# Cross-attention and routed experts on one core: a new call order, with stores spread and a bias moved

## The reference

```
h    = layernorm(x)
q,k,v = h Wq + bq, ctx Wk + bk, ctx Wv + bv            16 heads of 16
s    = alpha * 4 * (q.k) / (|q| + |k|)^2
x    = x + softmax(s) v Wo + bo
g    = layernorm(x);  p = softmax(g Wr)                8 experts
w    = the two largest of p, scaled to sum 1
x    = x + sum over the two chosen e of w_e (gelu(g W1[e] + b1[e]) W2[e] + b2[e])
```

## Time and profile before

| | us |
|---|---|
| median of 3 runs | 1087.3 (1085.24 to 1088.91) |
| the profiled execution, its own time | 1081.77 |
| its span, first to last instruction | 1080.0 |
| TensorE busy in the span | 957.4 (89%) |
| VectorE busy | 700.8 (65%) |
| ScalarE busy | 586.2 (54%) |
| GpSimd busy | 455.0 (42%) |

### The profile page before, as it was taken

The page is one execution under the profiler, slowest core; times in us unless marked ns, Lnnn a source line. Parts: engine busy times, 40 slices in busy tenths (PEclk is TensorE's granted clock), DMA queues, the critical chain, the costliest instruction groups (busy, mean ns, idle before and its releaser), DMA issues. The chain is left out here.

```text
span 1080.0 us, 27856 instructions
## 1 busy us (share of the span) xinstructions
PE 957.4 (89%) x9394; PEld 822.2 (76%) x9394; DVE 700.8 (65%) x1777; ACT 586.2 (54%) x978; POOL 455.0 (42%) x579
## 2 busy tenths in 40 slices
PE   2799999989989989899897159999999999999993
PEld 1588887867868868688676049889898989898982
DVE  5367787866867858668576436656666565656561
ACT  0478887976868758778585033433333333434340
POOL 4225548555564665544545401333333333323232
PEclk9699999998989989899899569999999999999997
DMA  4202223222231333233314456333332333233222
GB/s 131 75 27 80 66 80 106 81 66 71 80 105 32 129 124 114 73 109 103 129 25 170 120 190 259 61 61 54 49 52 46 57 48 54 46 49 55 26 26 25
DMA packets 64437, 87.86 MB, mean 81 GB/s; under 512 B 9360, under 2 KB 57872, under 8 KB 62128
## 3 DMA queue, kind: packets, MB, share of 16 engines
q1 hardware_dynamic: 48016, 64.95, 18.7%
q0 software_dynamic: 14304, 18.92, 10.7%
q10 hardware_dynamic: 1984, 2.21, 0.8%
HBM read 50.94 MB, written 34.06 MB: 79 GB/s over the span
## 5 line engine op out<-in xcount | busy, mean ns | idle before, releaser
L1415 POOL DMA_INDIRECT out<-yw,rb x78 | 132.8, 1703 | 321.6 <-DVE yw L1384 147.7
L1343 ACT ACTIVATE h<-s_ps,b1t,inv 128x256 f32<-128x256 f32 x156 | 79.5, 560 | 232.3 <-PE s_ps L1299 229.6
L1367 DVE SCALAR_TENSOR_TENSOR hs<-h,hsc,hs 128x512 f16<-128x512 f32 x156 | 117.5, 753 | 5.6
L1299 PE MATMUL s_ps<-xt,w1s 128*128 128x256 f16 x936 | 109.5, 274 | 0.0
L1299 PE MATMUL u_ps<-xt,w1s 128*128 128x256 f16 x936 | 108.6, 273 | 0.0
L648 ACT ACTIVATE pt<-gen,escale 128x512 f32<-128x512 f32 x128 | 85.8, 682 | 41.2 <-PE gen L434 20.8
L1314 PE MATMUL pv_ps<-w2s_sb,hs 128*128 x960 | 108.1, 273 | 0.0
L902 DVE SCALAR_TENSOR_TENSOR tw<-th,s_ps 128x1024 f32<-128x1024 f32 x64 | 77.9, 1217 | 38.5 <-PE s_ps L417 20.8
L1314 PE MATMUL gen<-w2s_sb,hs 128*128 x912 | 102.7, 273 | 0.0
L1314 PEld LDWEIGHTS pv_ps<-w2s_sb,hs 128*128 128x128 f16 x960 | 93.9, 98 | 10.9
L1365 DVE TENSOR_SCALAR hs<-h,hsc 128x512 f16<-128x512 f32 x156 | 76.5, 490 | 36.4 <-ACT h L1343 27.0
(11 more groups left out here) (234 smaller groups left out, 1798.6 us busy)
## 6 DMA issues: line engine op xcount, KB each, us to landing
wl<-L_ffn_W SPq DMA_DIRECT2D x16, 1024.0 KB, 5.9
rb<-xrec SPq DMA_DIRECT2D x39, 265.0 KB
w2s<-wst SPq DMA_DIRECT2D x8, 1024.0 KB, 8.8
w2s_sb<-w2s SPq DMA_DIRECT2D x8, 1024.0 KB, 16.6
xin<-x SPq DMA_DIRECT2D x32, 128.0 KB, 3.7
cin<-ctx SPq DMA_DIRECT2D x32, 128.0 KB, 2.1
xres<-x SPq DMA_DIRECT2D x32, 128.0 KB, 4.2
out<-x SPq DMA_DIRECT2D x32, 128.0 KB, 2.0
```

Of the source, the lines that this page charges most:

```text
L1299: ins = pe.matmul(hbank[q][:, o:o + SLOT], w, xt[s % 2][:, xp, k, :], start=(t == 0), stop=(t == len(terms) - 1))
L1343: ins = act.activation(h32[q][:, m % HB, :], hbank[q][:, o:o + SLOT], ACT.Gelu, scale=inv1[:, bass.ds(ex, 1)].bitcast(F32), bias=b1t[:, ba ...
L1367: dve.scalar_tensor_tensor(lo, h, scale, hi, ALU.mult, ALU.subtract).then_inc(sig("lo"), 1)
L1415: pool.indirect_dma_start(out[:, :], bass.IndirectOffsetOnAxis(ap=rb[j][:, i, D + NE:D + NE + 1], axis=0), yw[s % 2][:, i, :], None, compu ...
```

## The change

In the diff, in five parts:

1. `scatter(t, i, p)` issues one store; its eight calls stand at eight places of GpSimd's loop, with `scatter(0, 0)` at the end of one turn and the other seven spread over the next.
2. `add_bias` and `xb` go. bo is split in three bf16 parts (`bop`), and `project_out` begins with a product of ones with `bop` into the same bank. VectorE prepares `bop` at the start.
3. ctx is passed to the kernel with tokens in the columns; `cin` is then used by `project` as it is, in two buffers for each b, and TensorE's `norm` turns x alone.
4. `counts` is a function of its own, called before `shares`; `racc` comes before `rtok` in the chain of semaphore counts.
5. `TURNS` and the loops of all five engines have a new order.

```diff
 def norm(b, p):
     g = pe_turn(pe, f"xct{b}", p)
     pe.wait_ge(*at(f"xn{b}", p + 1))
-    pe.wait_ge(*dma(f"ldc{b}", p + 1))
-    for i, src in enumerate((xn[b], cin[b])):
-        for k in range(DC):
-            o = (DC * i + k) * P
-            ins = pe.transpose(g[:, o:o + P], src[:, k * P:(k + 1) * P], idf[:, :])
+    for k in range(DC):
+        ins = pe.transpose(g[:, k * P:(k + 1) * P], xn[b][:, k * P:(k + 1) * P], idf[:, :])
 def project(b, p):
...
-    for i, w in ((0, wq_sb), (1, wk_sb)):
-        for k in range(DC):
-            ins = pe.matmul(g[:, i * D:(i + 1) * D], xct[b][:, DC * i + k, :], w[:, k, :], ...)
+    for k in range(DC):
+        pe.matmul(g[:, 0:D], xct[b][:, k, :], wq_sb[:, k, :], start=False, stop=False)
+    pe.wait_ge(*dma(f"ldc{b}_{p % 2}", p // 2 + 1))
+    for k in range(DC):
+        ins = pe.matmul(g[:, D:2 * D], cin[b][:, p % 2, k, :], wk_sb[:, k, :], ...)
 def project_out(b, p):
     g = pe_turn(pe, f"wo{b}", p)
+    pe.matmul(g[:, 0:D], ones_b[0:RROWS, :], bop[:, :], start=True, stop=False)
     pe.wait_ge(*at("ote", 2 * p + b + 1))
```

SyncE's turn, and the part of VectorE's turn that reads from it:

```diff
 for it in range(-3, NP + 1):          # SyncE; each call guarded by its own range
-    load(1, it + 2)
-    load_weights(it)
+    residual(0, it)
+    store_x1(0, it - 1)
     store_w2(it - 1)
-    residual(1, it)
+    load_weights(it)
     load(0, it + 3)
-    residual(0, it + 1)
-    store_x1(0, it - 1)
     flat_rows(it + 1)
     store_x1(1, it - 1)
+    residual(1, it)
+    load(1, it + 3)
```

More of the change, by code:

```diff
@@ L90, in build @@
     turns = [(what, it + d, freed, (it + d) // 2 + 1 if what == "rank" else it + d + 1 if b is None else 2 * (it + d) + b + 1)
-             for it in range(-1, NP + 3) for what, d, freed, b in TURNS
+             for it in range(-1, NP + 4) for what, d, freed, b in TURNS
              if 0 <= it + d < NP and (what != "rank" or (it + d) % 2)]
@@ L505, in weight_sum @@
                 pe.matmul(g[:, 0:1], ones_f[:, :], wss[:, :], start=True, stop=True).then_inc(sig("wsum"), 1)
-            for it in range(-1, NP + 3):
+            for it in range(-1, NP + 4):
+                if 0 <= it - 1 < NP:
+                    stack(1, it - 1)
                 if 0 <= it - 2 < NP:
                     turn_on(0, it - 2)
+                    turned(2, 1, it - 2)
+                if 0 <= it - 4 < NP and it % 2:
+                    ranks(it - 4)
                 if 0 <= it - 1 < NP:
@@ L552, in tensor_program @@
                 if 0 <= it - 1 < NP:
-                    weight_products(it - 1)
-                    values(1, it - 1)
+                    turned(1, 1, it - 1)
+                    turned(2, 0, it - 1)
                 if 0 <= it - 2 < NP:
@@ L557, in tensor_program @@
                 if 0 <= it - 1 < NP:
-                    turned(2, 0, it - 1)
-                    turned(2, 1, it - 1)
-                if 0 <= it + 1 < NP:
-                    norm(1, it + 1)
+                    weight_sum(it - 1)
+                    values(1, it - 1)
                 if 0 <= it < NP:
+                    stack(0, it)
                     factors(0, it)
@@ L565, in tensor_program @@
                     logits(1, it - 2)
-                if 0 <= it - 3 < NP and it % 2 == 0:
-                    ranks(it - 3)
-                if 0 <= it < NP:
-                    stack(0, it)
                 if 0 <= it - 1 < NP:
-                    turned(3, 0, it - 1)
                     heads_back(0, it - 1)
-                    weight_sum(it - 1)
                 if 0 <= it < NP:
                     scores(0, it)
-                if 0 <= it - 1 < NP:
-                    turned(3, 1, it - 1)
             g = pe_turn(pe, "cnt", 0)
@@ L960, in choose, with counts @@
                 dve.tensor_tensor(rs["d"][:, :], rs["l2"][:, :], rs["l1"][:, :], ALU.subtract).then_inc(sig("rd"), 1)
+            def counts(p):
+                m = p // 2
+                if m:
+                    dve.wait_ge(*at("rank", m))
+                step(dve.tensor_tensor(hot[:, :, :], f("oh1"), f("oh2"), ALU.add))
+                step(dve.tensor_copy(acc2[:, 0, :], acc_cnt[:, :]))
+                for t in range(1, 4):
+                    step(dve.tensor_tensor(acc2[:, t, :], acc2[:, t - 1, :], hot[:, t - 1, :], ALU.add))
+                dve.tensor_tensor(acc_cnt[:, :], acc2[:, 3, :], hot[:, 3, :], ALU.add).then_inc(sig("racc"), 1)
             def shares(p):
@@ L1024, in weight_exponent @@
                 dve.tensor_scalar(wsc[:, :], wkk[:, :], -float(ONE), 268.0 * ONE, ALU.mult, ALU.add).then_inc(sig("wsc"), 1)
-            for it in range(-3, NP + 2):
+            for it in range(-3, NP + 3):
+                if 0 <= it < NP:
+                    squares(0, it)
+                    mantissas(it)
+                if 0 <= it - 2 < NP:
+                    residual(1, it - 2)
+                if 0 <= it < NP:
+                    logarithms(it)
+                if 0 <= it - 1 < NP:
+                    scores(2, it - 1)
+                if 0 <= it < NP:
+                    unit_coefficients(it)
+                if 0 <= it - 1 < NP:
+                    weight_diagonal(it - 1)
+                if 0 <= it - 2 < NP:
+                    logits(0, it - 2)
+                if 0 <= it < NP:
+                    rows(it)
+                if 0 <= it - 1 < NP:
+                    scores(3, it - 1)
+                    weight_exponent(it - 1)
+                if 0 <= it - 2 < NP:
+                    logits(1, it - 2)
+                if 0 <= it + 2 < NP:
+                    means(1, it + 2)
                 if 0 <= it - 1 < NP:
                     heads_back(0, it - 1)
-                    weight_exponent(it - 1)
+                if 0 <= it - 3 < NP and it % 2 == 0:
+                    shares(it - 3)
+                    positions(it - 3)
+                if 0 <= it - 2 < NP and it % 2:
+                    choose(it - 2)
                 if 0 <= it < NP:
@@ L1032, in vector_program @@
                 if 0 <= it - 1 < NP:
+                    residual(0, it - 1)
                     weight_low(it - 1)
-                    residual(0, it - 1)
+                if 0 <= it - 2 < NP and it % 2:
+                    counts(it - 2)
+                if 0 <= it + 1 < NP:
+                    squares(1, it + 1)
+                if 0 <= it - 1 < NP:
                     heads_back(1, it - 1)
```

262 lines of the change are left out of this document (119 added, 143 removed), and 16 rows, old and new, of the table TURNS.

## The result

The kernel after takes 1116.6 us (median of 4 runs, 1114.5 to 1119.8), the kernel before 1087.4 beside it (4 runs, 1085.2 to 1088.9): 1.027 times as long, 95 % interval 1.024 to 1.030. The forecast was 1110. The profiled execution took 1119.8 us by its own time, with a span of 1118.0 and a mean granted clock of 0.922 (before: 1081.8, 1080.0 and 0.939). That is +38.0 us, where the medians differ by 29.3: the profile of before is of an execution quicker than its median, that of after is the slowest of its four.

A forecast was written before the change was run, and what follows sets the result against it. TensorE was taken to bound stage one. Thirteen pairs of 36.55 us and two of 30.6 made 536.4 against 511.7, +24.7; start +2 and end −4 gave +22.7 on 1087.3: 1110 us, range 1055 to 1140.

The forecast's parts named there:

- The chain and the gap: Stage one: b=1's load, issued behind six flat-row transfers, delays heads_back and turn_on; 9.85 us chain, TensorE idle 2.75 per pair.
- The clean pair: Stage one, a pair without the gap: 30.34 us busy less 0.2, plus 0.45 for stores and small waits, 30.6.
- The clock: TensorE behind each gap: lower clock 0.50 for 10 us, seven times in ten, costing 4.6 us, 3.2 on average.
- the load of b = 0: SyncE: considered only in the VectorE rival, where this load, right behind the weight load, helped lengthen each pair by 2.4 us.
- The stores: GpSimd's block of eight scattered stores in stage one: spreading returns 40 of 42.9 us, leaving about 0.4 per group of eight.
- Start: Set-up: VectorE's eight-instruction split of the output bias ahead of the first statistics adds 2 us (1.2 to 3.4).
- End: End: counts ahead of shares, and earlier scattered stores off GpSimd's last normalisations, save 4 us (0 to 6).
- The sum: Whole kernel: intervals 536.4 against 511.7 us, +24.7; with start +2 and end −4, +22.7 on 1087.3, giving 1110.
- TensorE's work: Stage one: four context transposes go, two bias products come; net −0.2 us per pair, −3.5 in all.
- The rival in which the clock holds (1068): Stage one: the gap is there but the lower clock does not follow; 1068 us, faster; chance 0.22.
- the one in which VectorE's routing steps become the bound: Odd turns: choose and counts before heads_back(1), with VectorE's 3 us wait, lengthen each pair by 2.4 us; 1141; chance 0.14.

The follow-up runs named there:

- the kernel with both loads repaired: Kernel after with load(1, it+3) ahead of the flat rows, the b=0 x tile ahead of weight transfers, bias split in VectorE's turn 1: 1033.6 us, 0.991 times before.
- the kernel with the load first: Kernel after with one move on SyncE: load(1, it+3) issued ahead of the six flat-row transfers instead of behind them and two more transfers: 1072.5 us, 0.988 times before.
- the kernel with the load half-way: Kernel after with load(1, it+3) still behind the six flat-row transfers but ahead of store_x1(1) and residual(1): 1088.4 us, 0.999 times before.
- the plain block: Kernel before with scattered stores spread one by one, plus eight extra plain stores where the block of eight stood: 1043.7 us, 1.000 times before.

## Why the prediction was right, step by step

**The chain and the gap: right.** 9.85 us were worked out, 9.64 measured in the pair shown; 2.75 us per gap in thirteen intervals, 35.8 in sum, against 32.9 in thirteen gaps. Two errors cancel in this. Over all thirteen the chain took 10.3 us, 0.5 more, and TensorE's own work ahead of the gap 7.8 instead of 7.1. The two gaps of about 1 us are those of pairs in which TensorE was at 0.50 ahead of the gap, so that its own work took 9.3. Moving the load shows that it is the cause, and a part of the move takes away a part of the gap. The Trainium skill calls the time to issue a transfer usually small against the transfer ("DMA: Bandwidth & Descriptors", section "Issuing engines are not separate DMA queues"). This did not hold for these small transfers: the six issues of 3.68 us are the longest link of the chain.

**The clean pair: right.** 30.6 forecast; 30.63 on average in the kernel with both loads repaired, on chip B; 30.72 for an undisturbed pair on chip A.

**The clock: mis-sized in both directions.** Seven gaps in ten were to trip it at 4.6 us each, 3.2 on average, 41.6 in all. Eleven of the thirteen went with a stretch at 0.50 that began in the gap or up to 1.4 us behind it (the two of 0.97 and 0.98 us, at 448.53 and 530.60, did not), but the stretches were 3.4 or 6.8 us long, not 10: 51 us in sum, so at most 25.6 lost. The price had been taken from the block of stores, where further gaps, of 0.38 and 0.84 us, followed the one of 3.23; whether they made the stretch longer is not shown. The step from "over 2 us" to "a shorter one little but itself" left out the 1.51 us gap at 311.07.

**What the sum left out: the load of b = 0.** I had it in a rival, as part of a slower VectorE. It costs 12.3 us of gaps before L354 and 41 us at 0.50 around them, at most 20.5 lost. This omission filled what the clock had been given too much, so 536.4 us for the fifteen intervals came close to 540.6 partly by luck. Added up: 459.5 clean (chip B), 32.9 and 12.3 of gaps, leaves 35.9 for the clock and for what the chips differ in. The 92 us at half speed could have cost 46.

**The stores: right on chip A only.** 40 us were to come back, and alone they brought 40.3 (1087.9 to 1047.6). I called it a property of the block; it is one of stores in a row on chip A, and not of blocks of eight alone, as the blocks of three show there (ScalarE's copy up to 1.9 us late, where the prediction left 0.4 us per group). By the rule of the Trainium skill ("SBUF — State Buffer", section "SBUF: two separate sides"), as the prediction read it, nothing would have come back. Chip B agrees with that (235.84, no wait), the 40.3 us on chip A do not. Whether ScalarE's waits have anything to do with a port is not shown: no run here shows which resource made it wait.

**Start: +5.0 instead of +2.** The split took 2.5 us of VectorE (19.78 to 22.27 in the trace). The start of one and the same program varies, 38.11 and 40.14 in the two profiles of the kernel before, so the rest is best read on chip B, where three kernels ran: the first L378 stands at 40.14 before, 43.85 after and 40.88 with the split and both loads moved, and the first statistics at 20.77, 24.13 and 20.88. So 3.0 of the 3.7 us there went with the split, which had been put at 2, and 0.7 are left for the new order. The two profiles that the forecast is compared with show 1.3 us more than that.

**End: +4.1 instead of -4.** TensorE's last wait for the counts did get shorter (4.18 instead of 6.26 us), but the first transpose of stage two starts 86.0 us after the last L378, not 83.0; on chip B the ends are equal (532.3 and 532.2). Counts ahead of shares brought nothing that can be measured.

**The sum.** With these two terms off by +3 and +8 us, the profiles differ by 38.0 where 22.7 had been worked out; the medians, on which the forecast was given, differ by 29.3. That 1110 came within 7 us of 1116.6 owes something to this as well.

**TensorE's work: -3.5 forecast, -5.1 of busy time measured, nothing of it in the time.** The waits for VectorE's `ar` grew by 3.4.

The rival in which the clock holds (1068) was ruled out by the stretches at 0.50, and the one in which VectorE's routing steps become the bound by the kernel with the load first, where the gap ahead of `turn_on` is gone.

## What to carry to other kernels

When calls change their order, follow every load to the instruction that is queued behind its first reader: here one load, three calls too late on a queue that does no arithmetic, cost 4 %, and six small transfers ahead of it took longer to issue (3.68 us) than the tile took to land (2.33). The gaps of the kernel after, most of 2 to 4 us, cost 45 us themselves and about 36 more at half clock, so shortening such a gap can be worth more than its own length: with thirteen of them under 1.8 us the clock fell behind none in the execution profiled. That is no limit to rely on, since gaps of 1.4 and 1.5 us elsewhere were followed by half clock. A gain seen on one chip may be the removal of a loss that only that chip has: time the parts of a change apart, and on a second chip, before one part is allowed to pay for another.

## What was not expected of the hardware

- The same program took 1087.4 us beside the result and 1087.9 on chip A, and 1043.0 and 1043.4 on chip B. Between the two profiles nearly all of the difference lies in five intervals with a block of eight scattered stores, 40.7 of the 41.3 us (511.67 against 470.42 for the fifteen). In the profile of the kernel before, ScalarE waited 2.9 to 4.4 us inside five such blocks for products that TensorE's records show as done (at 235.78 for the exponential of 240.24), then TensorE had a gap of 1.5 to 3.4 us, then the clock fell. In the new order on chip A a block of eight did much less of this, 1.65 us at most, and in the kernel with the load first ScalarE's copy came 1.1 to 1.9 us late in blocks of three; in three of the six it started within 0.03 us of the end of the third store's issue. Why, stays open: no version of the old order with blocks of four ran on chip A, and the plain block was only seen on chip B.
- One moved issue changed the mean granted clock from 0.922 to 0.948.
- The ten runs of the kernel with the load half-way spread over 13 us (1078.0 to 1091.4), with mean clocks of 0.938 to 0.949, where the other kernels spread over 1 to 8.
